# The layer norm of the next block, cut into ten parts instead of six and spread over other steps of the feed-forward loop

## What is computed

```python
def ffn(x, w_gate, w_up, w_down):          # weights are int * (1/127)
    gate = jnp.einsum('bsd,hd->bsh', x, wg)
    up = jnp.einsum('bsd,hd->bsh', x, wu)
    h = jax.nn.silu(gate) * up
    return jnp.einsum('bsh,dh->bsd', h, wd)

x = x + attn(_layernorm(x))                # attn has its own layer norm and residual
x = x + ffn(_layernorm(x))                 # 4096 tokens per core, 1024 -> 3072 -> 1024
```

## Time and profile before

| | |
|---|---|
| runs of the kernel | 4459.52 and 4925.71 us (median 4692.62) |
| the profiled execution | 4455.75 us |
| its slowest core (5), first to last instruction | 4454.0 us |
| feed-forward part on core 5, first to last matmul | 2182.7 to 4441.2 us |
| TensorE busy, as the page counts it | 3662.0 us, 82% of the span |

### The profile page before, as it was taken

How to read it: one execution, slowest core, us unless ns; L and a number is a source line. 1 busy time by engine, 2 the same in 40 slices (tenths; PEclk the granted TensorE clock), 3 DMA queues, 4 the chain that set the end, 5 groups by cost and what they waited for, 6 DMA issues and landing times.

```text
span 4454.0 us, 61076 instructions; the slowest of 8 cores (4316.5 to 4454.0 us)
## 1 busy us (share of the span) xinstructions
PE 3662.0 (82%) x22544; PEld 2380.9 (53%) x22544; DVE 1259.7 (28%) x2998; ACT 657.7 (15%) x1083; POOL 184.8 (4%) x348
## 2 busy tenths in 40 slices
PE   6798897837287897865498988899888988899888
PEld 4343333337133433465376766676666766666666
DVE  4312212136423122154122322222222322222222
ACT  3212212110122222110001110111001101111100
POOL 0000000100000100000000000000000000000000
PEclk9897877767598998876699999999999999999999
DMA  4211111286323223389701101111011111110010
GB/s 124 62 53 59 64 45 45 69 172 197 113 81 99 71 78 80 114 185 188 134 28 39 39 26 42 46 37 36 27 48 39 39 35 33 48 37 33 29 41 10
DMA packets 275136, 306.05 MB, mean 69 GB/s; under 512 B 158229, under 2 KB 223893, under 8 KB 272026
## 3 DMA queue, kind: packets, MB, share of 16 engines
q1 hardware_dynamic: 115994, 136.42, 11.5%
q0 software_dynamic: 34944, 136.34, 9.7%
q10 hardware_dynamic: 123904, 29.40, 4.4%
HBM read 167.86 MB, written 136.31 MB: 68 GB/s over the span
## 4 chain that ended last, share of the span: by engine, by line
PE 68%; ACTq 11%; DVE 8%; DMA 4%; issue 4%; ACT 3%; another core or an unknown queue 1%; DVEq 0%; SPq 0%; POOLq 0%; POOL 0%
PE pb L1132 25%; PE pb L636 16%; PE pb L1101 13%; ACTq L94 11%; PE pb L574 9%; PE pb L797 2%; DVE h_st L873 1%; DMA h1n_stg<-s_h 1%; DVE n_t L539 1%; DMA s_h1n_lo<-lo_tok 1%; DVE xnT_lo L547 1%; DMA kTe<-s_kT 1%; ACT xnT_hi L544 1%; PE pb L387 1%
## 5 line engine op out<-in xcount | busy, mean ns | idle before, releaser
L1132 PE MATMUL pb<-hnT_hi_b,wgT 128*128 128x256 bf16 x3072 | 841.9, 274 | 55.6 <-DMA hnT_lo_b<-s_h1n_lo 51.1
L1132 PE MATMUL pb<-hnT_lo_b,wgT 128*128 128x256 bf16 x3072 | 841.4, 274 | 0.0
L1132 PE MATMUL pb<-hnT_hi_b,wuT 128*128 128x256 bf16 x3072 | 841.1, 274 | 0.0
L1132 PE MATMUL pb<-hnT_lo_b,wuT 128*128 128x256 bf16 x3072 | 840.3, 274 | 0.0
L1101 PE MATMUL pb<-wdT_t,hmT_hi 128*128 128x512 bf16 x1536 | 470.8, 389 | 199.7 <-DVE hmT_hi L1153 199.6
L1147 DVE SCALAR_TENSOR_TENSOR g_t<-pb,g_t 128x256 f32<-128x256 f32 x384 | 162.8, 424 | 1545.9 <-ACT g_t L1143 1481.4
L1101 PE MATMUL pb<-wdT_t,hmT_lo 128*128 128x512 bf16 x1536 | 471.1, 389 | 0.0
L1143 ACT ACTIVATE g_t<-pb 128x256 f32<-128x256 f32 x384 | 147.5, 384 | 1741.7 <-PE pb L1132 1449.2
L1132 PEld LDWEIGHTS pb<-hnT_hi_b,wgT 128*128 128x128 bf16 x3072 | 302.4, 98 | 138.4 <-issue 66.7
L1132 PEld LDWEIGHTS pb<-hnT_lo_b,wgT 128*128 128x128 bf16 x3072 | 302.2, 98 | 75.7 <-issue 4.2
L574 PE MATMUL pb<-wvT_hi,xnT_hi 128*128 128x512 bf16 x512 | 196.1, 473 | 176.2 <-DVE v_stg L604 169.8
(11 more groups left out here) (147 smaller groups left out, 3483.5 us busy)
## 6 DMA issues: line engine op xcount, KB each, us to landing
x_r<-x SPq DMA_DIRECT2D x32, 512.0 KB, 4.8
s_r<-r_r POOLq DMA_DIRECT2D x32, 512.0 KB, 5.5
s_v<-v_stg POOLq DMA_DIRECT2D x32, 512.0 KB, 3.2
s_qT<-qT_stg POOLq DMA_DIRECT2D x64, 256.0 KB, 2.9
s_kT<-kT_stg POOLq DMA_DIRECT2D x64, 256.0 KB, 2.9
kTe<-s_kT SPq DMA_DIRECT2D x16, 1024.0 KB, 7.0
v_p<-s_v SPq DMA_DIRECT2D x16, 1024.0 KB, 7.8
qT_c<-s_qT SPq DMA_DIRECT2D x32, 512.0 KB, 8.6
```

Source lines behind the costliest of these rows:

```text
L1132: hc=hc, bsl=bsl, st=st, sp=sp: e.matmul(pb[bnk][:, 0:256], wtt[:, d, hc * 128:(hc + 1) * 128], xt.ap()[:, bsl, d, :], start=st, stop=sp),
```

## The change

`p_stats` loses its square root, which becomes a part of its own, `p_sqrt`. `p_apply` loses ScalarE's copy of the hi part, which becomes `p_hi`. The ten parts are called in other steps, the two parts of a pair always in different ones: statistics of tile 0 in step 4 (was 8), square root 6 (8), apply 8 (10), hi 10 (10), store 12 (12); of tile 1 statistics 13 (13), square root 15 (13), apply 17 (15), hi 19 (15), store 21 (17); the transposing loads 22 (20). No operation is added or removed.

```diff
@@ p_stats
-                mag = P.op("vector", lambda e, fbn=fbn, fb=fb: e.bn_aggr(
-                    out=fstat[:, fb + 12:fb + 14], in_=fbn), waits=[mb1, mb2])
+                st[("ag", tc)] = P.op("vector", lambda e, fbn=fbn, fb=fb:
+                                      e.bn_aggr(out=fstat[:, fb + 12:fb + 14],
+                                                in_=fbn), waits=[mb1, mb2])
+            return f
+
+        def p_sqrt(tc):
+            def f():
+                fb = 20 * tc
                 st[("sr", tc)] = P.op("scalar", lambda e, fb=fb: e.activation(
                     out=fstat[:, fb + 14:fb + 15], in_=fstat[:, fb + 13:fb + 14],
-                    func=AF.Sqrt, bias=feps[:]), waits=[mag, m_feps])
+                    func=AF.Sqrt, bias=feps[:]),
+                    waits=[st[("ag", tc)], m_feps])
@@ p_apply
...
+        def p_hi(tc):
+            def f():
                 st[("hi", tc)] = P.op("scalar", lambda e: e.activation(
                     out=hi_tok[:], in_=h1n_stg[:, 1, :], func=AF.Copy),
-                    waits=[mh1n])
+                    waits=[st[("h1n", tc)]])
@@ the order and the steps
-        return [p_stats(0), p_apply(0), p_store(0),
-                p_stats(1), p_apply(1), p_store(1)]
+        return [p_stats(0), p_sqrt(0), p_apply(0), p_hi(0), p_store(0),
+                p_stats(1), p_sqrt(1), p_apply(1), p_hi(1), p_store(1)]
...
-            ln_sched = {8: [pcs[0]], 10: [pcs[1]], 12: [pcs[2]],
-                        13: [pcs[3]], 15: [pcs[4]], 17: [pcs[5]],
-                        20: [lambda bb=b + 1: emit_hnT_loads(bb)]}
+            ln_sched = {4: [pcs[0]], 6: [pcs[1]], 8: [pcs[2]],
+                        10: [pcs[3]], 12: [pcs[4]], 13: [pcs[5]],
+                        15: [pcs[6]], 17: [pcs[7]], 19: [pcs[8]],
+                        21: [pcs[9]],
+                        22: [lambda bb=b + 1: emit_hnT_loads(bb)]}
```

More of the change, by code:

```diff
@@ L947, in f @@
                     op0=OP.mult, op1=OP.mult), waits=[mrc])
[L948 to L953, removed]
+                st[("h1n", tc)] = P.op("vector", lambda e, fb=fb:
+                                       e.tensor_scalar(
+                                           out=h1n_stg[:, 1, :],
+                                           in0=h1n_stg[:, 0, :],
+                                           scalar1=fstat[:, fb + 15:fb + 16],
+                                           scalar2=fstat[:, fb + 16:fb + 17],
+                                           op0=OP.mult, op1=OP.add),
+                                       waits=[mnb] + ln_stg["prev_hi"])
+            return f
+        def p_hi(tc):
+            def f():
                 st[("hi", tc)] = P.op("scalar", lambda e: e.activation(
                     out=hi_tok[:], in_=h1n_stg[:, 1, :], func=AF.Copy),
-                    waits=[mh1n])
+                    waits=[st[("h1n", tc)]])
                 ln_stg["prev_hi"] = [st[("hi", tc)]]
```

## The result

The changed kernel takes 4417.95 us in the median of 11 runs, the kernel before 4482.64 us in the median of 10. So taken, the ratio is 0.9894 with a 95% interval of 0.9852 to 0.9936: 47 us (28 to 66) less, within 2%. Forecast was -14 us. The sign and the places were right; the size was a third of what the ratio says and, as the traces show, half of what the change itself gives.

A forecast was written before the change was run, and what follows sets the result against it. TensorE was taken as the bound, except where a wait breaks its 5.22 us beat. The terms -23.1 + 12.7 - 3.6 = -14.0 us took the profiled 4455.75 us to about 4442 us, range 4420 to 4474.

The forecast's parts named there:

- Waits of step 13: TensorE's waits ahead of step 13's down matmuls go, with uncounted time and half-clock loss behind them: -23.1 us.
- Square roots in steps 6 and 15, copies, statistics in step 4: On ScalarE and VectorE, the moved operations fit within the slack and cost nothing.
- The long wait moves and stays: TensorE's wait for the 16 transposing DMAs moves from step 20 to step 22; 0 us in the first place.
- Handover of the store: Ahead of Silu 22, tile 1's later store delays the transposes by 0.9 us a block: +12.7 us.
- the landing decides: Rival: in ScalarE's queue ahead of Silu 22, the store's landing becomes the deciding wait; 4476 us, chance 0.12.
- SP's load beside the transposes: SP's next load now starts with the transposes; taken as 0, bounds 0 and +45 us; as a rival, chance 0.04.
- End of the block: Step 23's down matmuls take 1.73 instead of 1.99 us, as Silus 22 and 23 come back to back: -3.6 us.
- I take no change: TensorE's half clock behind the long wait stays the same; ends 24 us either way.

The follow-up runs named there:

- sqrt_only: Kernel before with only the square root of tile 1 moved, from step 13 to step 14; ratio 0.9962 to the kernel before.
- loads_only: Kernel before with only the 16 transposing DMAs moved, from step 20 to step 22; ratio 0.9995 to the kernel before.
- late_store: Changed kernel with the store of tile 1 in step 22, directly ahead of the transposing DMAs; ratio 1.0134 to the kernel before.
- spread2: Changed kernel with the layer norm in steps 1 to 11 and transposing DMAs two at a time in steps 13 to 20; ratio 0.9442 to the kernel before.
- sp_queue: Changed kernel with tile 1 in steps 14 to 17 and the loop's 16 transposing DMAs issued by SP in step 18; ratio 0.9418 to the kernel before.
- early_store: Changed kernel with tile 1 worked off in steps 14 to 17, its store five steps ahead of the transposing DMAs; ratio 0.9925 to the kernel before.
- spread8: Changed kernel with the layer norm in steps 1 to 11 and transposing DMAs eight at a time in steps 13 and 17; ratio 0.9693 to the kernel before.

## Why the prediction was right or wrong

The changed kernel was forecast faster, and within 2%, and is both. The forecast of 4442 us, made against the profiled execution of 4455.75 us, is too high: less the 30.4 us of the traces it would have been 4425, inside the range of 4420 to 4474; the median of 4417.95 lies 2 us below the lower end, and the profiled execution after took 4412.52. The range left too little for the part before the loop, which differs by tens of microseconds from execution to execution; the forecast took 0.1%.

- **Waits of step 13: right.** -23.1 us forecast (17.5 waits, 2.2 uncounted, 3.4 clock, of core 5). `sqrt_only` measured 25.5, 21.3 of it waits in the mean of the cores. Some other cores had longer ones than core 5: 20.6 against 17.5 us on core 0 in the count of the forecast.
- **Square roots in steps 6 and 15, copies, statistics in step 4: right, nothing.** The Silu behind a square root is 1.28 us late, and TensorE doesn't wait.
- **The long wait moves and stays: right.** This is the step that made the forecast small, and the lists of waits show it.
- **Handover of the store: right in kind, a little too dear.** +12.7 forecast, +10.3 measured in the waits, 10.7 against the kernel with the early store. The first transpose starts 1.07 us behind Silu 21 in most blocks, 0.8 us later behind its Silu than before. The forecast took 2.56 us for the mean handover (I find 2.59 in the same rows, which leaves the 0.9 us as it is); in the 13 handovers of tile 1 in the trace after, it lies between 2.42 and 2.45 us, with no stragglers, which makes 2 of the 2.4 us. Why none are late there, while they reach 3.6 us in `loads_only` and `sqrt_only`, stays open. `late_store` shows what the rival "the landing decides" would have looked like, 81 us slower; its condition did not arise.
- **SP's load beside the transposes: right, nothing.** The 16 transposes take 20.57 us on average in core 5 after and 20.60 before.
- **End of the block: the term that was mis-sized.** "-3.6 us" was for the down matmuls of step 23 alone, and the rest that holds them fell by 4.5. The break of 0.47 us ahead of the next block's first gate matmul, in plain sight in the timeline and in the list of waits, was taken to stay. It goes as well, -6.9 us, in every kernel whose long wait stands in step 22, and in none of the others (`sqrt_only`, `spread2`, `sp_queue` keep it). So the forecast listed one of two breaks at a block's end. The semaphore checks in the traces of TensorE's queue, which no view above prints, show the cause. Ahead of that matmul the queue checks the 16 semaphores of the transposing DMAs one after another, 0.11 us each and about 1.7 us in all, and it begins with them right behind its last check for `hmT_lo` of step 23. In the kernels that keep the break the last check ends 0.06 us before the matmul starts, in every block read: the matmul waits for the checks. In those that lost it, the checks are over 0.9 to 2.7 us earlier, because `hmT_lo` of step 23 is there in time behind the long wait: the queue begins with them 3.3 to 3.6 us ahead of the matmul on average, instead of 1.8. How much of that is the half clock, which leaves the queue more time before the matmuls are through, no run separates.
- **"I take no change" for the clock behind the long wait: wrong by about -5 us.** Half-clock work fell by 8.2 us, of which 3.4 were in the first term. It differs from kernel to kernel (33.3, 31.8, 29.9, 28.0, 25.1 and 30.4 us for before, `loads_only`, `sqrt_only`, `early_store`, after and `late_store`) and doesn't follow the length of the wait. It lies inside the bound of 24 us that the forecast kept; what sets it stays open.

From -14.0 the differences lead to the account: -6.9 (block starts), -4.8 (clock beyond the 3.4), -2.4 (store), -1.5 (waits of step 13, 21.2 against 19.7) and -0.9 (step 23) make -30.5.

## What to carry to other kernels

Before asking what an instruction costs on an engine, look at what stands behind it in the same queue: here a square root of 0.29 us in each block cost 25 us in all because it waited for a load ahead of a Silu, and in each block 16 DMA issues of 1.24 us cost 200 us in all because they stood in one piece ahead of another. An engine that sits in the chain has a budget for extra work between two of its deadlines (here the beat of 5.22 us plus some 3 us of slack); work cut into portions under that budget was free here (two and four issues at a time), portions above it were not (eight). A wait of another engine's making is best kept out of that queue. And where a change removes the small waits beside a large one, take the large one apart first.

## What the runs showed of the hardware that was not expected

- A table load waits for the semaphores of the activation behind it. At 2526.10 us it starts only when TensorE's matmuls are done, although ScalarE had been idle for 3.15 us. So it is for all 28 table loads for Silu in blocks 1 to 14 of the changed kernel (88.7 us of waits on TensorE together): the 1.28 us of the load come on top of the wait.
- TensorE's clock falls behind far shorter waits than the long one: with waits of about 2.3 us twice a block (`spread8`) the half-clock work cost 19.9 us in 14 blocks; with none (`spread2`, `sp_queue`) the clock in blocks 1 to 14 never fell on any core.
- A transposing DMA costs the issuing queue 1.24 us on ScalarE and 1.16 us on SP; from one issue to the next it is 1.27 and 1.25 us, so the queues differ little.
- A wait for 16 DMAs that have long landed is not free: TensorE's queue takes about 1.7 us to check 16 semaphores one by one, and 0.47 us a block of it showed as a break where the queue was not ahead of the engine.
- The granted clock has stretches of 0.81 before the loop, 0 to 424 us long in sum on one of the cores compared here, for the same instructions; they move the start of the loop by tens of microseconds between executions.
